# Softmax row sums of a decoder layer: one 128x32-block reduction on VectorE and one small matmul in place of five transposes, and the last two halves' sums taken from GpSimd

## The chip, the core and the metric

One NeuronCore of a Trainium2 chip runs the whole layer. TensorE (PE; its weight loads are shown as PEld) does matmuls and transposes into PSUM, ScalarE (ACT) and VectorE (DVE) read PSUM and SBUF, GpSimd (POOL) here works on SBUF alone, and SyncE (SP) issues nearly all DMAs. Each engine runs its own program in order and waits on semaphores. The metric is the device time of one execution in microseconds (us). A difference of less than about 0.2% can't be told from none for this kernel.

## What is computed

```python
x = layernorm(x + self_attention(x))
kv = concatenate([context, x], axis=1)              # 1601 + 256 rows, 4 batches
q = rms_norm(x @ Wq); k = rms_norm(kv @ Wk); v = kv @ Wv
# 8 key/value heads of width 128, 4 query heads on each
scores = einsum('bhgqd,bhkd->bhgqk', q, k) / sqrt(128)
probs = softmax(scores, axis=-1)
x = layernorm(x + einsum('bhgqk,bhkd->bhgqd', probs, v) @ Wo)
x = layernorm(router_ffn(x))                        # 64 experts, top 8
```

The change touches the denominator of `softmax`: for each query, the sum of the exponentials over all 1857 keys.

## The kernel before

**Tiles, halves, units.** A unit is one key/value head of one batch (`UNITS` 32, index `v`). Each has two halves (`HALVES` 64, index `p`): two query heads times 256 queries, so 512 columns. The 1857 keys are `NJ` 15 tiles (`j`) of 128 rows, the last of 65. A score tile `t = 15 p + j` has keys on the partitions and queries along the row, so a softmax sum runs across partitions and over 15 tiles.

**The order.** It is written by hand as steps `s`, one score tile each, and every engine goes through the same steps in its own program. At step `s`: PE does `scores(s)`, then the jobs of `fill(s)`, then `pv(s - 20)`. ACT does `exp(s - 18)` (twice for most tiles: `P_hi` rounded, then the full value into `row`), then `copy_scores(s)`. DVE does `shift(s - 18)` (subtracts the maximum spread in `Mb_ps`), `raise_max(s - 1)` and drains the PSUM results of the step before. POOL does `lo(s - 18)` (`P_lo` = full value minus `P_hi`) and `add(s - 18)`. Two score banks tie PE to DVE: `scores(s)` waits for `raise_max(s - 2)`. A ring of 21 score rows ties all to POOL: `copy_scores(s)` waits until tile `s - 21` was split and added. Tiles in `FULL` (j = 6, 7, 14 in the last two batches) are not split: they cost POOL no `lo`, and PE one fp32 matmul (two passes) in place of three.

**The fill jobs** repeat every 30 steps; `c = (s + 20) mod 30` is the place in this cycle. Projections of keys (`KV`) and queries (`Q`), transposes of keys (`KT`) and queries (`QT`), the maximum (`MT`), and output projections (`O`, p, t) stand there. They take turns in two PSUM banks `F_ps`, and a job waits until the second one before it is drained. Projections for the last unit end before step 940, score tiles end at 959, the last `pv` stands in step 979.

**Row sums.** POOL adds 15 tiles into `acc[p % 2]` (L902 the first pair, L906 the others): 14 instructions of 128x512 a half. Job `AT` (L1130, step 15 p + 35, c = 10 or 25) has PE transpose `acc` in four pieces; DVE reduces the result to `sums` 128x4 (L1730) and takes the reciprocal `rinv` (L1732). Job `RT` (L1137, two steps later) transposes `rinv` to 4x128; DVE copies it to `rrow` (L1752), SP stores it (L733) and reads it back spread over all partitions as `rinv_spread` (L740). `divide(p)` (L1815) and `OT_low(p)` (L1819) on DVE, with ACT's `OT_high` between, make the operands of `O`. After the last `O` come the layer norm, the router and the store of the last batch, one after the other.

## Time and profile before

| | |
|---|---|
| median of 3 runs | 2812.35 us (2811.64 to 2814.04) |
| the profiled execution | 2814.29 us, of which the instructions span 2812.5 us |
| PE busy | 2717.2 us, 97% |
| POOL busy | 2353.4 us, 84% |
| DVE busy | 2123.2 us, 75% |
| ACT busy | 2101.7 us, 75% |
| mean granted TensorE clock | 0.986 of 2.4 GHz |

The shares are averages over the whole program. PE is nearly full until about 2660 us; after that POOL is, and from 2767 us on the program is a single chain of short steps. A matmul's shown duration overlaps the next one's, so its cost is the distance between starts. The same holds, by some 0.1 us, for DVE and ACT.

### The profile page before, as it was taken

To read this page: it belongs to the slowest core of one execution; us is meant where nothing else is said; L and a number is where in the kernel's file an instruction comes from. 1 tells how busy PE (TensorE), PEld (TensorE's weight loads), DVE (VectorE), ACT (ScalarE), POOL (GpSimd) and SP (SyncE) were. 2 spreads that over 40 slices of the span, in tenths; PEclk is the share of its full clock that TensorE was granted. 3 is DMA by queue.
4 is the path that set the end of the run, shared out by engine and by line. 5 is a ranking of instruction groups with operands and counts; after the bars stand their busy time and mean duration, and the time that the engine had idled before them with its cause. 6 is when DMAs were issued, how large, how long until landed. Compare 5 with 4: busy or idle time off the path is not lost.

```text
span 2812.5 us, 48040 instructions
## 1 busy us (share of the span) xinstructions
PE 2717.2 (97%) x14812; PEld 2218.6 (79%) x14812; DVE 2123.2 (75%) x3532; ACT 2101.7 (75%) x4201; POOL 2353.4 (84%) x2320
## 2 busy tenths in 40 slices
PE   7899999999999999999999999999999999999975
PEld 5778778777878888888888888888888888888853
DVE  5577787877777877777777877777777878787873
ACT  3587777777777778777778887787787778777761
POOL 4299999898788888878889888888898888888893
PEclk9999999999999999999999999999999999999995
DMA  7656565565555454555545555554455445344310
GB/s 234 237 196 212 198 210 199 200 216 185 171 188 202 158 179 164 182 180 197 178 152 189 169 184 176 181 184 160 159 174 173 154 160 179 127 162 150 117 42 26
DMA packets 159435, 485.65 MB, mean 173 GB/s; under 512 B 16839, under 2 KB 27849, under 8 KB 159182
## 3 DMA queue, kind: packets, MB, share of 16 engines
q1 hardware_dynamic: 157592, 481.01, 50.9%
q8 instruction: 121, 1.98, 0.3%
q10 hardware_dynamic: 1590, 1.58, 0.2%
q14 instruction: 132, 1.08, 0.1%
HBM read 403.09 MB, written 79.43 MB: 172 GB/s over the span
## 4 chain that ended last, share of the span: by engine, by line
PE 82%; POOL 7%; issue 5%; DVE 3%; ACT 2%; DMA 1%; SPq 0%; ACTq 0%; POOLq 0%; DVEq 0%
PE K_ps L971 9%; PE K_ps L973 9%; PE K_ps L972 9%; PE OT_ps L1001 7%; PE S_ps L971 7%; PE S_ps L973 7%; PE S_ps L972 7%; PE OT_ps L971 5%; PE OT_ps L972 5%; PE OT_ps L973 5%; POOL acc L906 4%; PE F_ps L971 2%; PE F_ps L972 2%; PE F_ps L973 2%; POOL P_lo L888 2%
## 5 line engine op out<-in xcount | busy, mean ns | idle before, releaser
L906 POOL TENSOR_TENSOR acc<-acc,scores 128x512 f32<-128x512 f32 (+1 forms) x832 | 1105.3, 1328 | 53.0 <-ACT scores L1323 25.4
L888 POOL TENSOR_TENSOR P_lo<-scores,P_hi 128x512 fp32r<-128x512 f32 x672 | 891.8, 1327 | 215.4 <-ACT scores L1323 214.5
L1663 DVE SCALAR_TENSOR_TENSOR running_max<-S_ps,rk,running_max 128x512 f32<-128x512 f32 (+1 forms) x896 | 669.7, 747 | 304.7 <-ACT scores L1309 302.2
L1309 ACT ACTIVATE scores<-S_ps,rk 128x512 f32<-128x512 f32 (+1 forms) x960 | 652.5, 680 | 139.6 <-PE S_ps L973 121.3
L1647 DVE TENSOR_TENSOR scores<-scores,Mb_ps 128x512 f32<-128x512 f32 (+1 forms) x960 | 648.7, 676 | 135.5 <-PE Mb_ps L1127 135.4
L1322 ACT ACTIVATE P_hi<-scores 128x512 fp32r<-128x512 f32 x672 | 422.9, 629 | 265.3 <-DVE scores L1647 183.6
L1323 ACT ACTIVATE scores<-scores 128x512 f32<-128x512 f32 (+1 forms) x960 | 596.6, 622 | 15.2 <-DVE scores L1647 12.8
L971 PE MATMUL S_ps<-QT_hi,KT_hi 128*128 128x512 f32 (+1 forms) x960 | 496.2, 517 | 11.9 <-DVE running_max L1663 10.1
L971 PE MATMUL K_ps<-Wkv_hi,kvT 128*128 128x256 f32 (+1 forms) x1664 | 470.4, 283 | 2.4 <-DVE kvT L1713 2.4
L973 PE MATMUL K_ps<-Wkv_hi,kvT 128*128 128x256 f32 (+1 forms) x1664 | 470.7, 283 | 0.0
L972 PE MATMUL K_ps<-Wkv_lo,kvT 128*128 128x256 f32 (+1 forms) x1664 | 469.6, 282 | 0.0
L973 PE MATMUL S_ps<-QT_hi,KT_lo 128*128 128x512 f32 (+1 forms) x960 | 379.8, 396 | 0.0
L972 PE MATMUL S_ps<-QT_lo,KT_hi 128*128 128x512 f32 (+1 forms) x960 | 378.6, 394 | 0.0
L971 PEld LDWEIGHTS K_ps<-Wkv_hi,kvT 128*128 128x128 f32 (+1 forms) x1664 | 310.2, 186 | 22.5 <-DVE kvT L1713 2.9
L972 PEld LDWEIGHTS K_ps<-Wkv_lo,kvT 128*128 128x128 f32 (+1 forms) x1664 | 310.1, 186 | 20.2
L971 PE MATMUL OT_ps<-P_hi,V_hi 128*128 128x512 f32 x672 | 289.8, 431 | 31.0 <-POOL P_lo L888 30.6
L973 PEld LDWEIGHTS K_ps<-Wkv_hi,kvT 128*128 128x128 f32 (+1 forms) x1664 | 310.4, 187 | 0.0
L1001 PE MATMUL OT_ps<-scores,V_full 128*128 128x512 f32 (+1 forms) x576 | 297.7, 598 | 0.0
L971 PEld LDWEIGHTS S_ps<-QT_hi,KT_hi 128*128 128x128 f32 (+1 forms) x960 | 177.6, 185 | 114.1 <-DVE running_max L1663 44.5
L972 PE MATMUL OT_ps<-P_lo,V_hi 128*128 128x512 f32 x672 | 266.1, 396 | 0.0
L973 PE MATMUL OT_ps<-P_hi,V_lo 128*128 128x512 f32 x672 | 265.6, 395 | 0.0
L972 PEld LDWEIGHTS S_ps<-QT_lo,KT_hi 128*128 128x128 f32 (+1 forms) x960 | 178.2, 186 | 93.5 <-issue 64.7
(226 smaller groups left out, 4637.5 us busy)
## 6 DMA issues: line engine op xcount, KB each, us to landing
kvT<-kvT_scratch SPq DMA_DIRECT2D x403, 512.0 KB, 3.8
Wq_hi<-weight_halves_scratch SPq DMA_DIRECT2D x48, 512.0 KB, 5.3
Wq_lo<-weight_halves_scratch SPq DMA_DIRECT2D x48, 512.0 KB, 6.6
Wo_hi<-weight_halves_scratch SPq DMA_DIRECT2D x48, 512.0 KB, 4.7
Wo_lo<-weight_halves_scratch SPq DMA_DIRECT2D x48, 512.0 KB, 5.7
kvT_scratch<-built SPq DMA_DIRECT2D x45, 512.0 KB, 4.4
rinv_spread<-rinv_scratch SPq DMA_DIRECT2D x64, 256.0 KB, 4.9
Wkv_hi<-weight_halves_scratch SPq DMA_DIRECT2D x24, 512.0 KB, 5.6
```

Source lines behind the costliest of these rows:

```text
L888: e.tensor_tensor(P_lo[n % PB][0:r, :], prob(t)[0:r, :], f(P_hi[n % PB][0:r, :]), ALU.subtract)\
L906: e.tensor_tensor(a[0:r, :], a[0:r, :], prob(t)[0:r, :], ALU.add).then_inc(s_acc, 1)
L971: e.matmul(out, l_hi, r_hi, start=first, stop=False)
L972: e.matmul(out, l_hi, r_lo, start=False, stop=False)
L973: return e.matmul(out, l_lo, r_hi, start=False, stop=last)
L1001: ins = e.matmul(OT_ps[:], V_full[v % 2][0:r, FULL[v].index(j), :], row[t % RING][0:r, :], start=first, stop=last)
L1309: e.activation(row[s % RING][0:r, :], S_ps[s % 2][0:r, :], ACT.Copy, scale=rk[0:r, v % 2, j:j + 1])\
L1322: e.activation(P_hi[n % PB][0:r, :], d, ACT.Exp)
L1323: e.activation(d, d, ACT.Exp).then_inc(s_p, 1)
L1647: e.tensor_tensor(d, d, Mb_ps[0:r, :], ALU.add).then_inc(s_d, 1)
L1663: e.scalar_tensor_tensor(a, src, k, a, ALU.mult, ALU.max).then_inc(s_top, 1)
```

## The change

**In every half** `RT` is gone, and `AT` is another job. DVE reduces `acc` (in SBUF, 128x512) straight to `block_totals` 128x16: `tensor_reduce` over 32 columns at a time with `apply_transpose=True`, which turns each 32x32 block first, so that the sum runs over 32 keys for each of 512 queries. This stands in DVE's step before `AT`'s (`sum_blocks`). PE then multiplies `block_totals` with `same_in_block` (128x32, ones where partition and column agree modulo 32), which adds the four groups of partitions: one fp32 matmul with a 16x32 result. DVE takes its reciprocal into `rrow` 16x32. Store, spread, `divide`, `OT_high` and `OT_low` stand two steps earlier.

**In half 62** six tiles (j = 2, 4, ..., 12) are no longer added by POOL; DVE reduces each by blocks (`sum_tile`, in the step after the exponential) into a part of `sq`, which the sums of squares no longer need. **In half 63** this holds for all 15 tiles, and ACT zeroes the unused rows of the last tile's buffer once. A short reduction over the 7 or 15 partial results (`sum_blocks`) makes `block_totals`.

**Output projections.** `O` of half 61 moves from steps 961 and 963 to 959 and 960, `O` of half 62 from 981 and 983 to 975 and 976. The loads of `Wo` that follow them on SP move too (L686).

```diff
+    SUMMED = [[] for p in range(HALVES - 2)] + [[2, 4, 6, 8, 10, 12], list(range(NJ))]
+    ADDED = [NJ * p + j for p in range(HALVES) for j in range(1, NJ) if j not in SUMMED[p]]
+    LATE = [p for p in range(HALVES) if len(SUMMED[p]) == NJ]
+    ADD_AT = {t: n for n, t in enumerate(ADDED)}
...
-            12: [("RT", 2 * v - 3)],
...
-            27: [("RT", 2 * v - 2), ("QT", v, 1)],
+            27: [("QT", v, 1)],
...
+        if v == UNITS:
+            jobs = [x for x in jobs if x[0] != "O" or x[1] != HALVES - 3]
+            jobs += {19: [("O", HALVES - 3, 0)], 20: [("O", HALVES - 3, 1)]}.get(c, [])
+        if v == UNITS + 1:
+            jobs = [x for x in jobs if x[0] != "O" or x[1] != HALVES - 2]
+            jobs += {5: [("O", HALVES - 2, 0)], 6: [("O", HALVES - 2, 1)]}.get(c, [])
...
-        return [x[1] for x in fill(s - 6) if x[0] == "RT"]
+        return [x[1] for x in fill(s - 6) if x[0] == "AT"]
...
-        chunk = {5: ("Wkv", v + 1, 0), 11: ("Wq", v + 1, 0), 13: ("Wq", v + 1, 1), 14: ("Wo", v - 2, 1),
-                 24: ("Wo", v - 1, 0)}.get(c)
+        chunk = {5: ("Wkv", v + 1, 0), 11: ("Wq", v + 1, 0), 13: ("Wq", v + 1, 1), (7 if v > UNITS else 14): ("Wo", v - 2, 1),
+                 (21 if v == UNITS else 24): ("Wo", v - 1, 0)}.get(c)
...
+    def summed_tile(t):
+        return t % NJ in SUMMED[t // NJ]
...
+    BLOCKS = []
+    for s in STEPS:
+        if 0 <= s - WAIT - 1 < NS and summed_tile(s - WAIT - 1):
+            BLOCKS.append(s - WAIT - 1)
+        BLOCKS += [("acc", x[1]) for x in fill(s + 1) if x[0] == "AT" and SUMMED[x[1]] and x[1] not in LATE]
+    BLOCK_AT = {x: n for n, x in enumerate(BLOCKS)}
...
-        sums = sb("sums", [P, 2, 4])
-        rinv = sb("rinv", [P, 2, 4])
-        rrow = sb("rrow", [4, P])
+        sums = sb("block_totals", [P, 2, 16])
+        same = sb("same_in_block", [P, 32])
+        rrow = sb("rrow", [16, 32])
...
-                e.wait_ge(s_fr, F_AT["RT", p] + 1)
-                e.dma_start(rsd[p % 2].rearrange("(i q) -> i q", q=P), rrow[:]).then_inc(s_rd, 16)
+                e.wait_ge(s_fr, F_AT["AT", p] + 1)
+                e.dma_start(rsd[p % 2].rearrange("(i q) -> i q", q=32), rrow[:]).then_inc(s_rd, 16)
...
-                if j == 0:
+                if t not in ADD_AT:
...
-                        e.wait_ge(s_ff, F_AT["AT", p - 2] + 1)
+                        e.wait_ge(s_bt, p - 1)
...
-            def turn_sums(p):
-                e.wait_ge(s_acc, acc_no(NJ * p + NJ - 1))
+            def add_blocks(p):
+                if p == 0:
+                    e.wait_ge(s_same, 1)
+                e.wait_ge(s_bt, p + 1)
                 out = take(("AT", p))
-                for i in range(4):
-                    ins = e.transpose(out[:, i * P:(i + 1) * P], acc[p % 2][:, i * P:(i + 1) * P], ident[:])
-                ins.then_inc(s_ff, 1)
-
-            def turn_reciprocals(p):
-                e.wait_ge(s_ri, p + 1)
-                out = take(("RT", p))
-                e.transpose(out[0:4, 0:P], rinv[:, p % 2, :], ident[:]).then_inc(s_ff, 1)
+                e.matmul(out[0:16, 0:32], sums[:, p % 2, :], same[:], start=True, stop=True).then_inc(s_ff, 1)
...
+                    if summed_tile(t):
+                        e.wait_ge(s_bs, BLOCK_AT[t] + 1)
+                    else:
+                        e.wait_ge(s_acc, ADD_AT[t + 1 if t % NJ == 0 else t] + 1)
+                if r < P and p in LATE:
+                    e.activation(row[s % RING][TAIL // 32 * 32:P, :], row[s % RING][TAIL // 32 * 32:P, :], ACT.Copy,
+                                 scale=0.0).then_inc(s_z, 1)
+                    e.wait_ge(s_z, LATE.index(p) + 1)
...
+            e.reduce_sum(same[:], ident[:].rearrange("p (i a) -> p a i", a=32), AX.X).then_inc(s_same, 1)
...
-                    e.reduce_sum(sums[:, p % 2, :], out.rearrange("p (i k) -> p i k", k=P), AX.X).then_inc(s_fr, 1)
-                    e.wait_ge(s_fr, F_AT[job] + 1)
-                    e.reciprocal(rinv[:, p % 2, :], sums[:, p % 2, :]).then_inc(s_ri, 1)
+                    if p:
+
+                        e.wait_ge(s_rd, 16 * p)
+                    e.reciprocal(rrow[:], out[0:16, 0:32]).then_inc(s_fr, 1)
...
-                elif job[0] == "RT":
-                    p = job[1]
-                    if p:
-
-                        e.wait_ge(s_rd, 16 * p)
-                    e.tensor_copy(rrow[:], out[0:4, 0:P]).then_inc(s_fr, 1)
...
+            def sum_tile(t):
+                p, j = divmod(t, NJ)
+                e.wait_ge(s_p, t + 1)
+                e.tensor_reduce(blocks_of(p)[:, SUMMED[p].index(j), :], prob(t).rearrange("p (j a) -> p j a", a=32), AX.X,
+                                ALU.add, apply_transpose=True).then_inc(s_bs, 1)
+
+            def sum_blocks(p):
+                if p >= 2:
+
+                    e.wait_ge(s_ff, F_AT["AT", p - 2] + 1)
+                added = acc[p % 2][:].rearrange("p (j a) -> p j a", a=32)
+                if not SUMMED[p]:
+                    e.wait_ge(s_acc, ADD_AT[NJ * p + NJ - 1] + 1)
+                    e.tensor_reduce(sums[:, p % 2, :], added, AX.X, ALU.add, apply_transpose=True).then_inc(s_bt, 1)
+                    return
+                n = len(SUMMED[p])
+                if p in LATE:
+                    e.wait_ge(s_bs, BLOCK_AT[NJ * p + NJ - 1] + 1)
+                else:
+                    e.wait_ge(s_acc, ADD_AT[NJ * p + NJ - 1] + 1)
+                    e.tensor_reduce(blocks_of(p)[:, n, :], added, AX.X, ALU.add, apply_transpose=True).then_inc(s_bs, 1)
+                    e.wait_ge(s_bs, BLOCK_AT["acc", p] + 1)
+                    n += 1
+                e.reduce_sum(sums[:, p % 2, :], blocks_of(p)[:, 0:n, :].rearrange("p k j -> p j k"), AX.X).then_inc(s_bt, 1)
...
+                if 0 <= s - WAIT - 1 < NS and summed_tile(s - WAIT - 1):
+                    sum_tile(s - WAIT - 1)
+                for x in fill(s + 1):
+                    if x[0] == "AT":
+                        sum_blocks(x[1])
```

How this moves instructions is shown at three places. **PE**, an `AT` job in the middle of the program (the score and value matmuls around it are those of `scores` and `pv`), before:

```order
L973 MATMUL K_ps<-Wkv_hi,kvT 128x256
L1134 MATMUL F_ps<-ident,acc 128x128 x4
L971 MATMUL OT_ps<-P_hi,V_hi 128x512
L972 MATMUL OT_ps<-P_lo,V_hi 128x512
L973 MATMUL OT_ps<-P_hi,V_lo 128x512
```

and now:

```order
L995 MATMUL K_ps<-Wkv_hi,kvT 128x256
L1157 MATMUL F_ps<-same_in_block,block_totals 16x32
L993 MATMUL OT_ps<-P_hi,V_hi 128x512
L994 MATMUL OT_ps<-P_lo,V_hi 128x512
L995 MATMUL OT_ps<-P_hi,V_lo 128x512
```

One matmul stands where four transposes stood; the fifth, two steps later, has nothing in its place.

**DVE**, the sums of half 60 (L1647 and L1671 are `shift`, L1663 and L1687 `raise_max`), before:

```order
L1757 TENSOR_TENSOR y<-y,F_ps 128x512
L1647 TENSOR_TENSOR scores<-scores,Mb_ps 128x512
L1663 SCALAR_TENSOR_TENSOR running_max<-S_ps,rk,running_max 128x512
L1647 TENSOR_TENSOR scores<-scores,Mb_ps 128x512
L1663 SCALAR_TENSOR_TENSOR running_max<-S_ps,rk,running_max 128x512
L1730 TENSOR_REDUCE sums<-F_ps 128x4
L1732 RECIPROCAL rinv<-sums 128x4
L1719 TENSOR_TENSOR KT_lo<-F_ps,KT_hi 128x512
```

and now:

```order
L1776 TENSOR_TENSOR y<-y,F_ps 128x512
L1844 TENSOR_REDUCE block_totals<-acc 128x16
L1671 TENSOR_TENSOR scores<-scores,Mb_ps 128x512
L1687 SCALAR_TENSOR_TENSOR running_max<-S_ps,rk,running_max 128x512
L1671 TENSOR_TENSOR scores<-scores,Mb_ps 128x512
L1687 SCALAR_TENSOR_TENSOR running_max<-S_ps,rk,running_max 128x512
L1757 RECIPROCAL rrow<-F_ps 16x32
L1743 TENSOR_TENSOR KT_lo<-F_ps,KT_hi 128x512
```

The reduction moved two steps ahead, in front of two `raise_max`, and only a small reciprocal is left behind them.

**DVE in the last half**, around the division of half 62, before (nothing but `shift` stands there for the tiles of half 63):

```order
L1752 COPY rrow<-F_ps 4x128
L1647 TENSOR_TENSOR scores<-scores,Mb_ps 128x512 x5
L1815 TENSOR_TENSOR OT_n<-OT_n,rinv_spread 128x512
L1647 TENSOR_TENSOR scores<-scores,Mb_ps 128x512 x2
L1819 TENSOR_TENSOR OT_lo<-OT_n,OT_hi 128x512
```

and now:

```order
L1671 TENSOR_TENSOR scores<-scores,Mb_ps 128x512
L1834 TENSOR_REDUCE sq<-scores 128x16
L1859 TENSOR_TENSOR OT_n<-OT_n,rinv_spread 128x512
L1671 TENSOR_TENSOR scores<-scores,Mb_ps 128x512
L1834 TENSOR_REDUCE sq<-scores 128x16
L1671 TENSOR_TENSOR scores<-scores,Mb_ps 128x512
L1863 TENSOR_TENSOR OT_lo<-OT_n,OT_hi 128x512
L1834 TENSOR_REDUCE sq<-scores 128x16
L1671 TENSOR_TENSOR scores<-scores,Mb_ps 128x512
L1834 TENSOR_REDUCE sq<-scores 128x16
```

Each `shift` now has a block reduction beside it on DVE. On POOL half 62 has 12 `lo` and 8 adds where it had 12 and 14, and half 63 has 12 `lo` and no add.

## Rows read from the trace of the kernel before

**Rows 1.** Windows: us; busy us of PE, PEld, DVE, ACT, POOL; clock; DMA share, GB/s.

```profile
1300.00:1800.00 500.00, 499.72 (x2802) 418.08 (x2801) 384.43 (x633) 397.24 (x802) 438.48 (x441) 1.00 0.53 177
...
2700.00:2750.00 50.00, 37.35 (x133) 23.46 (x131) 36.16 (x50) 31.30 (x56) 49.28 (x40) 0.91 0.16 53
```

**Rows 2.** Waits of PE's weight loads, 300 to 2600 us: total, times, longest.

```profile
PEld S_ps L971 <- DVE running_max L1663: 38.1, 104, 2.3
```

**Rows 3.** Timeline of PE around AT and RT of half 33: start, duration, what.

```profile
1549.21 0.60 PE L1134 MATMUL F_ps<-ident,acc 128*128 128x128 f32 x4
1549.56 0.48 PE L971 MATMUL OT_ps<-P_hi,V_hi 128*128 128x512 f32 x1
1549.88 0.39 PE L972 MATMUL OT_ps<-P_lo,V_hi 128*128 128x512 f32 x1
1550.11 0.39 PE L973 MATMUL OT_ps<-P_hi,V_lo 128*128 128x512 f32 x1
...
1555.19 0.27 PE L1140 MATMUL F_ps<-ident,rinv 128*4 128x128 f32 x1
...
1555.53 0.40 PE L972 MATMUL OT_ps<-P_lo,V_hi 128*128 128x512 f32 x1
```

**Rows 4.** Timeline of PE, small fp32 matmuls of the router (8, two passes each).

```profile
2222.48 1.90 PE L1161 MATMUL F_ps<-self_qkv,w_stage 128*128 128x64 f32 x16
2224.19 0.48 PE L971 MATMUL OT_ps<-P_hi,V_hi 128*128 128x512 f32 x1
```

**Rows 5.** DVE's lines: duration ns min/median/max, first and last start us.

```profile
L1730 DVE TENSOR_REDUCE sums<-F_ps x64: 678/681/693, 178.2 to 2768.2; 128x4 f32<-128x512 f32 x64
...
L1671 DVE TENSOR_REDUCE ss_k<-sq x128: 541/679/689, 48.3 to 2674.5; 128x4 f32<-128x512 f32 x96, 128x3 f32<-128x384 f32 x32
...
L1815 DVE TENSOR_TENSOR OT_n<-OT_n,rinv_spread x64: 680/954/5920, 197.8 to 2778.1; 128x512 f32<-128x512 f32 x64
```

**Rows 6.** Timeline of POOL where it takes up half 62, and at its last split.

```profile
2699.34 2.54 POOL L888 TENSOR_TENSOR P_lo<-scores,P_hi 128x512 fp32r<-128x512 f32 x2
...
2762.66 1.25 POOL L888 TENSOR_TENSOR P_lo<-scores,P_hi 128x512 fp32r<-128x512 f32 x1
```

**Rows 7.** Timeline of DVE in halves 62 and 63 (idle before, and releaser).

```profile
2695.73 0.69 DVE L1647 TENSOR_TENSOR scores<-scores,Mb_ps 128x512 f32<-128x512 f32 x1 [3.23 <-PE Mb_ps L1127]
...
2703.41 0.66 DVE L1647 TENSOR_TENSOR scores<-scores,Mb_ps 128x512 f32<-128x512 f32 x1
2703.99 0.74 DVE L1663 SCALAR_TENSOR_TENSOR running_max<-S_ps,rk,running_max 128x512 f32<-128x512 f32 x1
2704.65 0.68 DVE L1757 TENSOR_TENSOR y<-y,F_ps 128x512 f32<-128x512 f32 x1
...
2729.63 1.28 DVE L1647 TENSOR_TENSOR scores<-scores,Mb_ps 128x512 f32<-128x512 f32 x2 [3.32 <-PE Mb_ps L1127]
...
2741.47 5.92 DVE L1815 TENSOR_TENSOR OT_n<-OT_n,rinv_spread 128x512 f32<-128x512 f32 x1 [1.31 <-DMA rinv_spread<-rinv_scratch]
```

**Rows 8.** Timeline of ACT, the exponentials of one tile in half 61.

```profile
2687.97 0.62 ACT L1322 ACTIVATE P_hi<-scores 128x512 fp32r<-128x512 f32 x1
2688.49 0.62 ACT L1323 ACTIVATE scores<-scores 128x512 f32<-128x512 f32 x1
```

**Rows 9.** Timeline of PE in half 63.

```profile
2743.20 0.80 PE L971 MATMUL OT_ps<-P_hi,V_hi 128*128 128x512 f32 x1 [0.85 <-POOL P_lo L888]
2743.79 0.63 PE L972 MATMUL OT_ps<-P_lo,V_hi 128*128 128x512 f32 x1
2744.22 0.63 PE L973 MATMUL OT_ps<-P_hi,V_lo 128*128 128x512 f32 x1
```

**Rows 10.** Timeline of all engines after the last tile.

```profile
2767.11 1.06 PE L1134 MATMUL F_ps<-ident,acc 128*128 128x128 f32 x4
...
2770.54 0.26 SPq L733 DMA_DIRECT2D rinv_scratch<-rrow  x1
...
2778.10 0.69 DVE L1815 TENSOR_TENSOR OT_n<-OT_n,rinv_spread 128x512 f32<-128x512 f32 x1 [5.33 <-DMA rinv_spread<-rinv_scratch]
```

More of the change, by code:

```diff
@@ L186, in real @@
                 return True
-            return 0 <= job[1] < (HALVES if job[0] in ("RT", "O", "MT", "AT") else UNITS)
+            return 0 <= job[1] < (HALVES if job[0] in ("O", "MT", "AT") else UNITS)
         return [x for x in jobs if real(x)]
     def divided(s):
-        return [x[1] for x in fill(s - 6) if x[0] == "RT"]
+        return [x[1] for x in fill(s - 6) if x[0] == "AT"]
     def splits(s):
@@ L301, in x_no @@
         return TILE_NO[b, n]
-    def acc_no(s):
-        p, j = divmod(s, NJ)
-        return (NJ - 1) * p + j
+    def summed_tile(t):
+        return t % NJ in SUMMED[t // NJ]
     def split_tile(t):
@@ L520, in layer @@
         s_mb = sem("negated_max_spread")
-        s_ri = sem("row_reciprocal")
+        s_same = sem("same_in_block")
+        s_z = sem("last_tile_rows_zeroed")
+        s_bs = sem("block_sums")
+        s_bt = sem("block_totals")
         s_rd = sem("row_reciprocals_stored")
@@ L561, in xrow_of, with blocks_of @@
             return row[0] if k < CTX and k % 2 else xrow[:]
+        def blocks_of(p):
+            at = p % 2 * 256
+            return sq[:].rearrange("p h d -> p (h d)")[:, at:at + NJ * 16].rearrange("p (k j) -> p k j", k=NJ)
         def bank(table, label):
@@ L807, in _ @@
                 for x in fill(s - 1):
-                    if x[0] == "RT":
+                    if x[0] == "AT":
                         store_reciprocals(x[1])
                 for x in fill(s - 3):
-                    if x[0] == "RT":
+                    if x[0] == "AT":
                         spread_reciprocals(x[1])
@@ L899, in add @@
                     if p >= 2:
-                        e.wait_ge(s_ff, F_AT["AT", p - 2] + 1)
+                        e.wait_ge(s_bt, p - 1)
                     e.tensor_tensor(a[:], prob(t - 1)[:], prob(t)[:], ALU.add).then_inc(s_acc, 1)
                     return
-                e.wait_ge(s_acc, acc_no(t - 1))
+                e.wait_ge(s_acc, ADD_AT[t])
                 e.tensor_tensor(a[0:r, :], a[0:r, :], prob(t)[0:r, :], ALU.add).then_inc(s_acc, 1)
@@ L1213, in _ @@
                     elif x[0] == "AT":
-                        turn_sums(x[1])
+                        add_blocks(x[1])
                     elif x[0] == "FR":
@@ L1224, in _ @@
                         mix(x[1], x[2])
-                    elif x[0] == "RT":
-                        turn_reciprocals(x[1])
                     else:
@@ L1307, in copy_scores @@
                         e.wait_ge(s_pv, t + 1)
-                    e.wait_ge(s_acc, acc_no(t + 1 if t % NJ == 0 else t))
+                    if summed_tile(t):
[6 more added lines that the diff above has]
+                    e.wait_ge(s_z, LATE.index(p) + 1)
                 e.activation(row[s % RING][0:r, :], S_ps[s % 2][0:r, :], ACT.Copy, scale=rk[0:r, v % 2, j:j + 1])\
@@ L1514, in _ @@
             e.wait_ge(s_pad, 5)
+            e.wait_ge(s_id, 2)
+            e.reduce_sum(same[:], ident[:].rearrange("p (i a) -> p a i", a=32), AX.X).then_inc(s_same, 1)
             e.wait_ge(sa_w, 32)
@@ L1837, in _ @@
                     OT_low(p)
+                if 0 <= s - WAIT - 1 < NS and summed_tile(s - WAIT - 1):
+                    sum_tile(s - WAIT - 1)
+                for x in fill(s + 1):
+                    if x[0] == "AT":
+                        sum_blocks(x[1])
                 for p in divided(s):
```

## The prediction

> **What bounds the kernel now.** I read the stretches first. In 500 us of the middle of the program PE is busy 499.72 us, POOL 438.48, ACT 397.24 and DVE 384.43, at the full clock [rows 1]: PE bounds, and its matmuls follow each other without a gap. PE is not alone, though: its weight loads waited 104 times, 38.1 us in all, for DVE's running maximum [rows 2]. In the last 50 us before 2750 this has turned: POOL is busy 49.28 of 50 us, PE only 37.35 [rows 1], and PE waits for `P_lo` before a value matmul [rows 9]. From 2767 us on a chain of single steps is left: turn the sums, invert, store, spread (a DMA that DVE waits 5.33 us for), divide, project, normalise, route [rows 10]. So there are three stages, and the change has a part in each.
>
> **Part 1: five transposes a half less on PE.** Without `AT` the first value matmul behind it would start at 1549.21 and the second 0.23 us later. They start at 1549.56 and 1549.88 [rows 3]. The second is 0.44 us late, and that is the cost of four transposes. For `RT` the second value matmul should start at 1555.42 and starts at 1555.53: 0.11 us. Together 0.55 us a half.
>
> The new matmul isn't in the trace. The nearest is the router's: 16 passes with 128 columns of weights and 64 moving take 1.71 us, 0.107 each [rows 4]. Two such passes and the 0.09 us that the first fp32r matmul behind a transpose loses (0.32 where 0.23 is usual, [rows 3]) make 0.30 us, an upper bound, since 16 columns of weights and 32 moving are less. The lower bound is one pass like `RT`'s, 0.11. I take 0.20, between. Net 0.345 us a half.
>
> It counts where PE bounds. Half 61's sum falls in POOL's stage, so 61 sums (0 to 60) count: 61 x 0.345 = **21 us** (15 to 27 by the bounds).
>
> What else moves here: DVE loses the PSUM reduction of 0.68 us [rows 5] with a reciprocal and a copy, and gains a reduction of `acc`, two steps earlier. The plain reduction of 128x512 from SBUF takes 0.679 us (L1671, [rows 5]); I take that for the block reduction. DVE ends a little less loaded. Queued behind the new wait for POOL's last add are `shift` and `raise_max`, on which PE's scores hang. The add is normally done two steps before, so I cost the wait at nothing; the cover is POOL's idle time of 61 us in the 500 [rows 1]. `acc` is 128x512 behind DVE's own `y` drain, and PE has 0.69 us of scores in front of `AT`: just enough for 0.6 us. `divide` and `OT_low` two steps earlier collide with other POOL instructions than now; 0.68 us alone, 0.954 in the median and 5.92 at worst [rows 5]. The DMA in front of `divide` keeps as many steps as it had. I cost both moves at nothing, since DVE has the idle time, but they take it at another place: plus or minus 8 us for the waits of part 1, because 38.1 us of them exist to be made smaller or larger.
>
> For the block reduction itself the Trainium skill, in Vector Engine (DVE) Microarchitecture Reference, section 3.8, says that the 32x32 array that transposes the input keeps one element per cycle per lane, which would leave the reduction at the price of the plain one. No row here shows it; if it holds, the rival of the slow reduction below falls.
>
> **Part 2: half 62 and half 63.** POOL takes up half 62 at 2699.34 [rows 6]. Before that, everything shifts by part 1.
>
> Half 62 up to the first `shift` of half 63: this `shift` waits for the spread maximum, which PE makes behind `pv` of tile j = 12 of half 62, hence behind its `lo`. POOL has 11 `lo` and 11 adds to there, 22 x 1.26 [rows 6] = 27.7 us, and the `shift` came at 2729.63 [rows 7], 2.6 us after that. Now it is 17 instructions, 21.4 + 2.6: 6.3 us less. But DVE has its own list from its first `shift` of half 62 at 2695.73: 15 `shift` at 0.6, 13 maxima at 0.66, 4 drains of `y` at 0.6 [rows 7], one reduction of the maximum and seven block reductions at 0.6, `divide` and `OT_low` at 1.1 each: 27.3 us, and some 2.5 us for the two banks of scores that it still waits on. That ends at 2725.5. So the saving is 2729.6 - 2725.5 = **4.1 us** (1.5 to 6.3).
>
> Half 63: from 2729.63 to the end of the last `lo`, 2763.91, it takes 34.3 us now, 26 POOL instructions. Without the adds DVE leads: a `shift` and a block reduction per tile, 1.2 us, 1.27 with the wait for the two exponentials (0.52 + 0.62, [rows 8]). 13 tiles x 1.27 = 16.5 us; the sums of half 62 (0.6 + 0.3) and a reciprocal, 1.1; `divide` 1.1 to 1.7 and `OT_low` 1.1, with 1 us of waiting for the DMA and ACT between them; one drain 0.6; then the last split tile's own way through `shift`, exponentials and `lo`, 0.7 + 1.2 + 1.3 with semaphores. That is 25 us, so **9.3 us** less (6 to 12). The `divide` of 5.92 us [rows 7] was DVE shut out by a POOL with a backlog of adds. Now POOL gets its work from DVE tile by tile and runs dry, so I don't expect it again. The first `O` of half 62 now waits on PE for `OT_low`, with the last `pv`s behind it. PE's 12 matmuls there were hidden in a DMA's time, and they are hidden again if PE has its full clock: 2.8 us in an idle engine. At half the clock, which the pitch of 0.43 us in [rows 9] shows for this place (0.23 is that of the full clock, [rows 3]), two `O` and four `pv` are 9 us, and up to 2.5 us stick out.
>
> ACT's zeroing of a few rows happens once: nothing, in ACT's idle time. So does the one small reduction that makes `same_in_block`, beside the loads of the opening. The moved `Wo` loads stand on SP before the store of the reciprocals, and their condition is met by then.
>
> **Part 3: behind the last tile.** From the end of the last `lo` to the store of the reciprocals 6.6 us pass now: 3.2 to the transposes at 2767.11 [rows 10], then four transposes, a reduction, a reciprocal, a transpose behind the first `O` of half 62, a copy behind a drain, and the store at 2770.54 [rows 10]. Now 3.2, one matmul (0.3) and one reciprocal (0.2): 3.7. Saved **2.9 us** (2 to 3.5). Store and spread stay at 7.6 us (2770.54 to 2778.10, [rows 10]), the rest as it was.
>
> **Sum.** 21 + 4.1 + 9.3 + 2.9 = 37.3 us off the execution's 2814.29 us: 2777.0. The span was 2812.5 us and the execution has 1.8 around it; the median of the runs is 1.9 us below this execution. On the median: 2812.35 - 37.3 = 2775 us, 1.3% faster.
>
> **Rivals.**
> - *The gain of part 1 is eaten by DVE* (2787 us). PE already waits for the maximum; a reduction of 0.6 us in front of two `raise_max`, and `divide` moved to another place among short steps, could take half of the 21 us, and DVE and PE at half the clock could leave the last halves 2 to 3 us worse than summed. For it: [rows 2]. Against: DVE has 116 us idle of 500 [rows 1] and has less to do.
> - *The new matmul costs only 0.11 and DVE's lighter load takes waits away* (2762 us): 27 us in part 1, 8 us of the 38.1, and 17 us in the rest. For it: waits stand where the old reduction stood before a drain of keys.
> - *The block reduction costs about twice a plain one* (2790 us): 0.6 us more, 21 times in the last halves, 12.6 us; in the batches it is just within the 0.7 us slack, some 2 us. Nothing in the trace excludes it, as no reduction there transposes.
> - *Slower: the block reduction takes 2.7 us, four times the plain one* (2898 us). Then DVE stops for 2 us more in every half; 0.7 of that is slack, and 61 x 1.3 = 79 us arrive at PE through the two score banks, and 21 x 2.04 = 43 us in the last halves; less the 37 us. It decides from an excess of about 1 us: 61 x 0.3 + 21 = 39 us cancel the gain.
> - *The change does not do what it says*: another engine holds the last halves, and part 1 is all below 0.2%. PE's full row of matmuls speaks against it.
>
> **How the numbers follow.** My forecast, 2766 to 2784 us, 0.50. Eaten by DVE 0.17; the larger gain 0.14; the twice-as-dear reduction 0.10; slower 0.05; no effect 0.04. The range that leaves out the slow case, no effect and the ends of the outer two is 2761 to 2792 us. Faster by over 0.2% (what a measurement of this kernel can tell from none): 0.91; within 0.2% 0.04; slower 0.05.
>
> **What the profile after would show.** Part 1: the second value matmul behind the new `AT` 0.2 us late in place of 0.44, and the same place of the program near 2600 us some 20 us earlier; its reduction at 0.68 us; waits for the running maximum near 38 us. Part 2: DVE, no longer POOL, nearly full in the last 40 us of tiles; the first `shift` of half 63 about 30 us behind half 62's; a `divide` under 2 us. Part 3: 3.7 us from the last `lo` to the store. I am wrong if the block reduction is much over 0.68 us, if PE shows new waits for `block_totals` or the maximum, or if PE at half the clock ends last in half 63.

## The result

| | |
|---|---|
| median of 4 runs | 2784.10 us (2781.45 to 2786.27) |
| the kernel before, 4 runs | 2811.99 us (2811.07 to 2814.04) |
| ratio | 0.9899, 95% interval 0.9887 to 0.9912 |

The changed kernel is 1.0% faster, by 27.9 us. The forecast was 2775 us, a gain of 37.3, and its range reached from 2761 to 2792.

The page's first part, busy time and share of the span, of the kernel after:

```profile
span 2782.6 us, 47574 instructions
...
PE 2699.7 (97%) x14620; PEld 2190.5 (79%) x14620; DVE 2126.8 (76%) x3491; ACT 2098.3 (75%) x4202; POOL 2326.1 (84%) x2300
```

Windows of after, with the columns of [rows 1]:

```profile
1300.00:1800.00 500.00, 499.67 (x2773) 414.44 (x2772) 380.81 (x623) 398.14 (x806) 438.81 (x440) 1.00 0.53 178
2700.00:2750.00 50.00, 36.29 (x125) 22.09 (x123) 40.04 (x66) 30.47 (x54) 31.45 (x25) 0.90 0.22 74
2720.00:2730.00 10.00, 7.91 (x20) 4.73 (x21) 8.99 (x16) 6.33 (x12) 7.99 (x7) 0.66 0.08 26
2730.00:2740.00 10.00, 8.26 (x30) 4.95 (x28) 9.43 (x16) 7.32 (x13) 6.45 (x5) 1.00 0.01 2
```

PE still fills the middle. In the last 50 us POOL has gone from 49.28 to 31.45 us busy, and near 2735 DVE leads with 9.43 of 10. That is the picture that the prediction drew. The sizes of its terms are another matter. The table takes each stretch from the same events in the two traces: the first `shift` of half 62 and of half 63, the end of the last `lo`, the store of the reciprocals, the division of half 63, the end of the span.

| stretch | before, us | after, us | gain | forecast |
|---|---|---|---|---|
| start to half 62 | 2695.73 | 2686.80 | **8.9** | 21 |
| half 62 | 33.90 | 30.38 | 3.5 | 4.1 |
| half 63, to the last `lo` | 34.28 | 24.15 | 10.1 | 9.3 |
| to the store | 6.63 | 2.44 | 4.2 | 2.9 |
| store to division | 7.56 | 4.36 | **3.2** | 0 |
| the rest | 34.4 | 34.5 | -0.1 | 0 |
| sum | | | 29.9 | 37.3 |

Three of the events of after, DVE's first `shift` of half 62 and of half 63, and POOL's last two `lo`:

```profile
2686.80 0.69 DVE L1671 TENSOR_TENSOR scores<-scores,Mb_ps 128x512 f32<-128x512 f32 x1 [2.81 <-PE Mb_ps L1149]
...
2717.18 1.28 DVE L1671 TENSOR_TENSOR scores<-scores,Mb_ps 128x512 f32<-128x512 f32 x2 [0.81 <-PE Mb_ps L1149]
...
2738.79 2.54 POOL L910 TENSOR_TENSOR P_lo<-scores,P_hi 128x512 fp32r<-128x512 f32 x2
```

Part 1 gave less than half of its 21 us, and 3.2 us came from a place that was to stay as it was. (29.9 is the difference of the two profiled spans, 27.9 that of the medians. Of the 8.9 us, 0.8 lie before score tile 20, where the two kernels still do the same: that is the spread of single profiles, and no gain.)

### The profile page after: what moved, and what is told of

The parts are those of the page before. It is cut to its first block, busy times and chain, and to the rows that moved or that the text cites. A ratio compares the mean times of both kernels' runs of the same rounds, so it can differ in the third digit from the quotient of the medians.

```text
span 2782.6 us, 47574 instructions
## 1 busy us (share of the span) xinstructions
PE 2699.7 (97%) x14620; PEld 2190.5 (79%) x14620; DVE 2126.8 (76%) x3491; ACT 2098.3 (75%) x4202; POOL 2326.1 (84%) x2300
## 4 chain that ended last, share of the span: by engine, by line
PE 78%; POOL 7%; issue 6%; DVE 5%; ACT 2%; DMA 1%; SPq 0%; POOLq 0%; DVEq 0%; ACTq 0%
PE K_ps L993 9%; PE K_ps L995 9%; PE K_ps L994 9%; PE OT_ps L1023 7%; PE S_ps L993 7%; PE S_ps L995 6%; PE S_ps L994 6%; PE OT_ps L993 5%; PE OT_ps L994 4%; PE OT_ps L995 4%; POOL acc L928 4%; POOL P_lo L910 2%; PE F_ps L993 2%; PE F_ps L994 2%; PE F_ps L995 2%
## 5 line engine op out<-in xcount | busy, mean ns | idle before, releaser
L928 POOL TENSOR_TENSOR acc<-acc,scores 128x512 f32<-128x512 f32 x813 | 1068.5, 1314 | 50.7 <-ACT scores L1345 23.3
L910 POOL TENSOR_TENSOR P_lo<-scores,P_hi 128x512 fp32r<-128x512 f32 x672 | 902.6, 1344 | 220.3 <-ACT scores L1345 219.2
L1687 DVE SCALAR_TENSOR_TENSOR running_max<-S_ps,rk,running_max 128x512 f32<-128x512 f32 (+1 forms) x896 | 668.0, 745 | 272.6 <-ACT scores L1331 270.0
L1671 DVE TENSOR_TENSOR scores<-scores,Mb_ps 128x512 f32<-128x512 f32 (+1 forms) x960 | 645.6, 673 | 138.9 <-PE Mb_ps L1149 138.8
L993 PE MATMUL S_ps<-QT_hi,KT_hi 128*128 128x512 f32 (+1 forms) x960 | 495.6, 516 | 15.5 <-DVE running_max L1687 13.8
```

Source lines behind the costliest of these rows:

```text
L910: e.tensor_tensor(P_lo[n % PB][0:r, :], prob(t)[0:r, :], f(P_hi[n % PB][0:r, :]), ALU.subtract)\
L928: e.tensor_tensor(a[0:r, :], a[0:r, :], prob(t)[0:r, :], ALU.add).then_inc(s_acc, 1)
L993: e.matmul(out, l_hi, r_hi, start=first, stop=False)
L1671: e.tensor_tensor(d, d, Mb_ps[0:r, :], ALU.add).then_inc(s_d, 1)
L1687: e.scalar_tensor_tensor(a, src, k, a, ALU.mult, ALU.max).then_inc(s_top, 1)
```

## The price of the new matmul

PE around `AT` of half 33 in the kernel after, the counterpart of [rows 3] (start, duration, what; a PEld row is the load of weights):

```profile
1551.01 0.28 PE L995 MATMUL K_ps<-Wkv_hi,kvT 128*128 128x256 f32 x1
1551.22 0.11 PEld L1157 LDWEIGHTS F_ps<-same_in_block,block_totals 128*16 128x16 f32 x2
1551.22 0.23 PE L1157 MATMUL F_ps<-same_in_block,block_totals 128*16 128x32 f32 x2
...
1551.38 0.50 PE L993 MATMUL OT_ps<-P_hi,V_hi 128*128 128x512 f32 x1
...
1551.72 0.39 PE L994 MATMUL OT_ps<-P_lo,V_hi 128*128 128x512 f32 x1
```

`K_ps` matmuls follow each other at 0.12 us, so the first value matmul would start at 1551.13 without the job and the second, 0.23 later, at 1551.36. It starts at 1551.72: **0.36 us**, where I had taken 0.20 and given 0.30 as the upper bound. `RT` had cost 0.11 and its going shows whole (step c = 12 is 0.10 to 0.11 us shorter in every batch). Net 0.19 us a half in place of 0.345: 61 x 0.155 = 9.5 us of the missing 12.

Two runs ask what the 0.36 is made of. The first issues the matmul twice:

```diff
+                e.matmul(out[0:16, 0:32], sums[:, p % 2, :], same[:], start=True, stop=True)
                 e.matmul(out[0:16, 0:32], sums[:, p % 2, :], same[:], start=True, stop=True).then_inc(s_ff, 1)
```

> The small fp32 matmul of `AT` is issued twice in a row. It says what it costs in the stream: the second value matmul behind it stands 0.36 us late in the changed kernel, where I had taken 0.20. If the two passes are the price (0.08 each) and the rest is paid once for entering and leaving, the place grows by 0.16 us and the whole by 8 to 10 us; if a weight load that can't be drawn ahead is paid each time, by 0.25 to 0.35 us and 15 to 20 us.

Measured: 2788.40 us (2787.85 to 2788.96, 2 runs), ratio 0.9914 (0.9894 to 0.9933). The same place of its trace:

```profile
1553.02 0.28 PE L995 MATMUL K_ps<-Wkv_hi,kvT 128*128 128x256 f32 x1
...
1553.30 0.22 PE L1158 MATMUL F_ps<-same_in_block,block_totals 128*16 128x32 f32 x2
...
1553.79 0.40 PE L994 MATMUL OT_ps<-P_lo,V_hi 128*128 128x512 f32 x1
```

The second value matmul is at 0.77 us behind the last `K_ps` where it was at 0.71. A second fp32 matmul, two passes, costs 0.06 us here and 0.07 in the mean of step c = 10, less than either expectation, and 61 of them are the 4.3 us between the medians of the two kernels. So 0.29 of the 0.36 isn't the passes: by this count it is paid for going into the fp32 matmul and out again.

The second run makes it one fp32r matmul, so that it is of the kind around it. `block_totals` and `same_in_block` are written as fp32r; the sums lose their low bits by this (the lines that permit the rounding are left out here):

```diff
-        sums = sb("block_totals", [P, 2, 16])
-        same = sb("same_in_block", [P, 32])
+        sums = sb("block_totals", [P, 2, 16], F32R)
+        same = sb("same_in_block", [P, 32], F32R)
```

> `block_totals` and `same_in_block` are written rounded as fp32r, so that the small matmul is one pass of the same kind as its neighbours (the sums lose low bits by it). The doubled matmul had shown that two passes themselves are 0.07 us of the 0.36. Theory C (the remaining 0.29 us is the change between fp32 and fp32r matmuls and their weight loads): the place falls to under 0.15 us, step c = 10 from 3.18 to about 2.95 us, and the whole by 12 to 18 us. Theory D (it is the wait on DVE's semaphore and the short weight load, whatever the type): c = 10 stays within 0.08 us of 3.18 and the whole falls by less than 5 us.

Measured: 2773.22 us (2771.61 to 2774.84, 2 runs), ratio 0.9855 (0.9835 to 0.9875), some 11 us below after, a little less than theory C's 12 to 18 and far from theory D. Its trace at the same place:

```profile
1544.15 0.28 PE L995 MATMUL K_ps<-Wkv_hi,kvT 128*128 128x256 f32 x1
1544.15 0.10 PEld L1157 LDWEIGHTS F_ps<-same_in_block,block_totals 128*16 128x16 f32 x1
1544.27 0.18 PE L1157 MATMUL F_ps<-same_in_block,block_totals 128*16 128x32 f32 x1
1544.27 0.19 PEld L993 LDWEIGHTS OT_ps<-P_hi,V_hi 128*128 128x128 f32 x1
...
1544.61 0.40 PE L994 MATMUL OT_ps<-P_lo,V_hi 128*128 128x512 f32 x1
```

Expected without the job is 1544.27 + 0.23 = 1544.50, and it is 1544.61: 0.11 us, my lower bound. (That bound was `RT`'s price; that the two agree to the digit is chance.) The load rows tell where the rest had been. As fp32r the small matmul's weights are loaded at 1544.15, while the `K_ps` matmul streams, and the value matmul's at 1544.27, with the small one. As fp32 both loads wait: the first until 1551.22, 0.21 behind the start of `K_ps`, and the next until 1551.38. That a matmul of another kind breaks the overlap of loads and matmuls twice is what the rows show; why is not shown.

This is the step of the prediction that failed. It took the price from the router's fp32 matmuls [rows 4], 0.107 a pass, and those 16 passes stand in a row. A row pays the way in and out once; that is read off the doubled matmul, and wasn't measured on the router's row itself. My 0.09 for the way out was right in kind and about a third of the whole.

## The division two steps earlier

The other part of the loss I had written down at nothing, "plus or minus 8 us". DVE's lines of after (duration ns min/median/max), as in [rows 5]:

```profile
L1859 DVE TENSOR_TENSOR OT_n<-OT_n,rinv_spread x64: 648/1092/2752, 191.3 to 2748.1; 128x512 f32<-128x512 f32 x64
...
L1844 DVE TRANSPOSE_TENSOR_REDUCE block_totals<-acc x62: 692/703/712, 173.7 to 2690.6; 128x16 f32<-128x512 f32 x62
```

The block reduction is 0.70 us, always (the 21 of single tiles in the last halves, too: 0.64 to 0.71). Of these 83 reductions 13 ran wholly inside a POOL instruction of over 1 us, and none took more than 0.71. The division is 2.75 us at times. In the first 16 halves the divisions took 14.6 us over 0.68 each, where before they took 4.5. One of them, DVE, POOL and PE in the kernel after:

```profile
743.44 2.38 POOL L967 TENSOR_TENSOR Wo_lo<-w_stage,Wo_hi 128x1024 fp32r<-128x1024 f32 x1 [0.80 <-ACT Wo_hi L1478]
...
743.62 2.75 DVE L1859 TENSOR_TENSOR OT_n<-OT_n,rinv_spread 128x512 f32<-128x512 f32 x1
...
746.89 0.74 DVE L1687 SCALAR_TENSOR_TENSOR running_max<-S_ps,rk,running_max 128x512 f32<-128x512 f32 x1
...
747.68 0.51 PE L993 MATMUL S_ps<-QT_hi,KT_hi 128*128 128x512 f32 x1 [0.94 <-DVE running_max L1687]
```

Up to 828 us POOL splits weights, 128x1024 in 2.38 us. The new step puts the division 0.18 us behind such a split. DVE is held past the end of it, the maximum behind the division is late, and PE stands 0.94 us for it. Both instructions read two operands from SBUF. The Trainium skill (SBUF — State Buffer, Who interferes with whom) says that a VectorE instruction with two SBUF inputs contends with a GpSimd one that reads SBUF, and that one with at most one such input, outside the 2-port modes, does not. The trace agrees on both: 2.75 and 0.70 us.

The experiment gives halves 0 to 60 their old steps for the division, `OT_high` and `OT_low`, and leaves the last three as changed:

```diff
-        return [x[1] for x in fill(s - 6) if x[0] == "AT"]
+        return [x[1] for x in fill(s - 8) if x[0] == "AT" and x[1] < HALVES - 3] \
+            + [x[1] for x in fill(s - 6) if x[0] == "AT" and x[1] >= HALVES - 3]
```

> The change as it is, but `divide`, `OT_high` and `OT_low` stand in their steps of before for halves 0 to 60 (c = 18 and 3 for the division). Theory A (the earlier steps of the division ate part of the gain): in the changed kernel the division of odd halves takes 2.75 us in the first batch, where 0.68 was usual, and the PE step c = 17 there grew from 2.20 to 3.41 us; undone, the time falls by 6 to 11 us, to 2773 to 2778 us, and c = 17 is back at 2.2 us. Theory B (the block reduction in front of two running maxima ate it, the division is only where the delay shows): the time stays within 2 us of 2784, and PE waits as much for the running maximum.

Measured: **2776.79 us** (2775.70 to 2777.12, 4 runs), ratio 0.9873 (0.9856 to 0.9889), 7.3 below after, as theory A had it. Of the same half the division is now

```profile
742.53 0.68 DVE L1860 TENSOR_TENSOR OT_n<-OT_n,rinv_spread 128x512 f32<-128x512 f32 x1
```

and half 62 starts at

```profile
2677.62 0.69 DVE L1672 TENSOR_TENSOR scores<-scores,Mb_ps 128x512 f32<-128x512 f32 x1 [3.24 <-PE Mb_ps L1150]
```

9.2 us before the 2686.80 of after. The steps tell where. I measured each step by the distance from the end of the third score matmul of one tile to that of the next, and took the mean over a batch (steps 40 to 219, 220 to 459, 460 to 699 and 700 to 929); of 30 steps, two halves:

| us for two halves | before | after | division late |
|---|---|---|---|
| batch 0 | 84.37 | 84.76 | 83.82 |
| batch 1 | 82.59 | 82.68 | 82.21 |
| batch 2 | 81.46 | 81.10 | 81.06 |
| batch 3 | 83.74 | 82.68 | 82.68 |
| batch 0, step c = 17 | 2.20 | 3.41 | 2.20 |
| batch 0, step c = 19 | 2.66 | 2.07 | 2.65 |
| every batch, c = 10 | 3.27 | 3.18 | 3.18 |
| every batch, c = 25 | 2.26 | 2.14 | 2.14 |

The division at c = 17 costs 1.2 us and gives 0.6 back at c = 19. Of the 9.2 us at half 62, 7.4 have come about by step 270 (838 us in after), where the splits of weights end. Some 2.5 more come after them, up to 1470 us, at c = 5 and 19, and 0.8 of it goes again towards the end; what delays those steps is open.

That DVE's reduction before two `raise_max` should cost something has fallen for batches 0 to 2: with the reduction in its new place and the division in its old one, c = 17 is 2.20 as before, and the steps c = 9 and 24, where the reduction stands, are as long as before to 0.02 us.

## The 6.5 us that nobody had asked for

With the division late half 62 starts 18.1 us before that of the kernel before, and 61 x 0.19 is only 11.6. The steps show where the other 6.5 came from: some 4.7 in batch 3, 1.0 in batch 0, and 0.8 in the opening, where the kernels are alike. Batch 3 gained 1.06 us for two halves, where the two jobs explain 0.38. It sits at c = 27, 2.80 to 2.26, and c = 28, 3.02 to 2.80, and in batch 0 at c = 27, 2.55 to 2.30. DVE at such a place before, at 2411 to 2416 us, behind `AT` at c = 25:

```profile
2411.68 0.68 DVE L1730 TENSOR_REDUCE sums<-F_ps 128x4 f32<-128x512 f32 x1
...
2412.49 0.66 DVE L1719 TENSOR_TENSOR KT_lo<-F_ps,KT_hi 128x512 fp32r<-128x512 f32 x1
...
2413.96 1.10 DVE L1808 TENSOR_TENSOR self_x<-self_x 128x128 f32<-128x128 f32 x1
2414.98 1.24 DVE L1810 TENSOR_SCALAR self_small<-self_small 128x2 f32<-128x2 f32 x1
```

and with the change (the kernel with the late division):

```profile
2398.42 0.34 DVE L1758 RECIPROCAL rrow<-F_ps 16x32 f32<-16x32 f32 x1
2398.69 0.61 DVE L1744 TENSOR_TENSOR KT_lo<-F_ps,KT_hi 128x512 fp32r<-128x512 f32 x1
...
2400.11 0.42 DVE L1828 TENSOR_TENSOR self_x<-self_x 128x128 f32<-128x128 f32 x1
2400.46 1.24 DVE L1830 TENSOR_SCALAR self_small<-self_small 128x2 f32<-128x2 f32 x1
```

DVE is full here: the router's work for one half of the queries stands behind the sums, and the next score tile hangs on its end. In the 4 us from 2411.5 DVE was busy 3.93 of 4. Before, this step took 3.97 us at tile 847, now 2.84. From the first of these rows to `KT_lo` it was 0.81 us and is 0.27: that is the reduction that left, less what the wider reciprocal adds, 0.54. From the router's product `self_x` to the next row it was 1.02 and is 0.35, 0.67 less: it has two SBUF operands, and before it started 0.33 us into a POOL split of 1.28 us and ended behind it; now it starts 0.28 us before one POOL instruction ends and is through at the seam to the next. The two make 1.21, a little more than the 1.13. To test it I put, on top of the late division, a reduction of the old shape back into the drain of `AT`, into a spare tile that nobody reads:

```diff
+                    e.reduce_sum(spare[:, 0, 0:4], out.rearrange("p (i k) -> p i k", k=P), AX.X)
```

> On top of late_divide (2776.8 us), DVE's reduction of 128x512 from PSUM stands again where it stood before, in the drain of `AT`, for nothing. Part 1 brought more than PE's own saving: with the late division half 62 begins 18 us earlier, and 61 x (0.55 - 0.36) is only 12. Theory E (the other 6 us are DVE's: without the reduction the running maxima behind it come sooner, and PE's steps c = 27 and 28 of the last batch are 0.75 us shorter a pair): 4 to 7 us come back, 2781 to 2784 us, and c = 27 of the last batch rises from 2.26 to 2.6 us or more. Theory F (they come from elsewhere, the missing `RT` for one): less than 2 us, c = 27 stays.

Measured: 2785.32 us (2782.42 to 2786.66, 3 runs), ratio 0.9899 (0.9880 to 0.9919), 8.5 above the kernel with the late division alone. The place in its trace:

```profile
2405.18 0.68 DVE L1759 TENSOR_REDUCE spare<-F_ps 128x4 f32<-128x512 f32 x1
...
2407.47 1.08 DVE L1830 TENSOR_TENSOR self_x<-self_x 128x128 f32<-128x128 f32 x1
```

The 1.08 is back, c = 27 is 2.89 in batch 3 and 2.79 in batch 0. The direction is confirmed. The size is more than expected: c = 28 of batch 3 rises to 3.14, where the kernel before had 3.02. The kernel has the wider reciprocal and the block reduction on DVE as well, which may be why; that isn't shown.

The next run, again on top of the late division, doubles the block reduction in halves 0 to 61 (a second copy goes to a spare tile); the short sums of the last two halves' tiles are not doubled. It asks how much slack (time that DVE can lose without PE waiting) there is in front of `AT`:

```diff
+                    e.tensor_reduce(spare[:, 1, :], added, AX.X, ALU.add, apply_transpose=True)
                     e.tensor_reduce(sums[:, p % 2, :], added, AX.X, ALU.add, apply_transpose=True).then_inc(s_bt, 1)
```

> On top of late_divide (2776.8 us), the block reduction of `acc` is done twice in halves 0 to 61, first into an unused tile: 0.7 us more of DVE in front of two running maxima, and `AT` waits for it. This is the batches' share of my rival of a reduction twice as dear, which I had put at 2 us because of 0.7 us of slack. If the slack is there, 1 to 4 us more (2778 to 2781). If PE's place behind `raise_max` has none, most of 61 x 0.7 us arrives: 20 to 40 us more.

Measured: 2785.60 us (2784.79 to 2787.68, 3 runs), ratio 0.9904 (0.9884 to 0.9923), 8.8 more than without. Neither expectation holds, and the steps say why. For two halves batch 0 is 83.82, batch 1 82.19 and batch 2 81.06, which is what it was to 0.02 us: 0.7 us more of DVE cost nothing there. Batch 3 is 84.14 against 82.68 (c = 25 +0.26, c = 27 +0.60, c = 28 +0.61), 7 x 1.46 = 10.2 us. (The rest of the 12.0 us between the two profiled spans is 2.1 us in the opening, where the kernels are alike, and 0.6 in half 62, less 0.9 behind the last tile.) So the slack of "just enough" is there in the first three batches, and DVE has none in batch 3.

## The last halves

Two runs take the parts apart. The first leaves POOL all its additions:

```diff
-    SUMMED = [[] for p in range(HALVES - 2)] + [[2, 4, 6, 8, 10, 12], list(range(NJ))]
+    SUMMED = [[] for p in range(HALVES)]
```

> The change with POOL adding all tiles of all halves again (no tile is reduced by itself on DVE); the reduction of `acc` by blocks, the small matmul and the moved steps stay. If the last halves' gain (some 13 us up to the last `P_lo`) comes from POOL's 20 missing adds, the time rises by 12 to 15 us, to 2796 to 2799 us, and POOL is full to the end of half 63. If it comes from the moved output projections and divisions, it rises by less than 4 us.

Measured: 2799.57 us (2798.57 to 2802.49, 4 runs), ratio 0.9955 (0.9940 to 0.9970), 15.5 above after. Its division of half 62 is stretched again:

```profile
L1859 DVE TENSOR_TENSOR OT_n<-OT_n,rinv_spread x64: 677/1107/7558, 193.3 to 2763.7; 128x512 f32<-128x512 f32 x64
```

7.56 us at worst, 5.92 before [rows 5], 0.65 after:

```profile
2728.93 0.69 DVE L1834 TRANSPOSE_TENSOR_REDUCE sq<-scores 128x16 f32<-128x512 f32 x1
...
2730.12 0.69 DVE L1834 TRANSPOSE_TENSOR_REDUCE sq<-scores 128x16 f32<-128x512 f32 x1
2730.74 0.65 DVE L1859 TENSOR_TENSOR OT_n<-OT_n,rinv_spread 128x512 f32<-128x512 f32 x1
```

The pitch of `shift` and block reduction is 1.2 us a tile, as summed. So POOL's backlog was the bound of half 63, and its additions are worth 15.5 us together with what they do to the division: by the profiles 4.0 in half 62, 9.6 in half 63 and 1.8 from the last `lo` to the store. The late division with three more tiles (8, 10, 12 of half 61) summed by DVE:

```diff
-    SUMMED = [[] for p in range(HALVES - 2)] + [[2, 4, 6, 8, 10, 12], list(range(NJ))]
+    SUMMED = [[] for p in range(HALVES - 3)] + [[8, 10, 12], [2, 4, 6, 8, 10, 12], list(range(NJ))]
```

> Late division, and three tiles (j = 8, 10, 12) of half 61 are summed on DVE as well. POOL takes up half 62 behind half 61's adds; if POOL still bounds half 61, three adds of 1.26 us less bring 2 to 4 us (2773 to 2775 us). If DVE or PE bounds there by now, nothing, or up to 2 us more.

Measured: 2773.92 us (2772.94 to 2774.69, 4 runs), ratio 0.9857 (0.9841 to 0.9874): 2.9 below the two-half version, which ran on another chip, with intervals that overlap. In the profiled executions half 62 starts 1.3 us earlier and the last `lo` ends 0.7 earlier. A gain of a microsecond or two is likely, not proved.

The second part undone is the place of the output projections and of the `Wo` loads:

```diff
-        if v == UNITS:
-            jobs = [x for x in jobs if x[0] != "O" or x[1] != HALVES - 3]
-            jobs += {19: [("O", HALVES - 3, 0)], 20: [("O", HALVES - 3, 1)]}.get(c, [])
-        if v == UNITS + 1:
...
-        chunk = {5: ("Wkv", v + 1, 0), 11: ("Wq", v + 1, 0), 13: ("Wq", v + 1, 1), (7 if v > UNITS else 14): ("Wo", v - 2, 1),
-                 (21 if v == UNITS else 24): ("Wo", v - 1, 0)}.get(c)
+        chunk = {5: ("Wkv", v + 1, 0), 11: ("Wq", v + 1, 0), 13: ("Wq", v + 1, 1), 14: ("Wo", v - 2, 1),
+                 24: ("Wo", v - 1, 0)}.get(c)
```

> The change with the output projections of halves 61 and 62, and the loads of `Wo` that follow them, in their steps of before. In the changed kernel the spread of the last reciprocals took 4.4 us from store to division, 7.6 before. Theory A: the loads of `Wo` (two of 512 KB) ran beside the spread before; with the old steps they do so again, and 2.5 to 4 us come back (2786.5 to 2788), with a store to division of about 7.5 us. Theory B: the layout of 16 rows of 32 makes the store quick; then it stays near 4.4 us and the time within 1.5 us.

Measured: 2789.44 us (2786.15 to 2790.90, 4 runs), ratio 0.9916 (0.9901 to 0.9930), 5.3 above after. It is not where I looked: the time from store to division stays, as theory B had it, though its reason fails too. All engines after the last tile, kernel after (SPq is SP's queue, where DMAs are issued):

```profile
2743.13 0.23 PE L1157 MATMUL F_ps<-same_in_block,block_totals 128*16 128x32 f32 x2
...
2743.77 0.32 SPq L755 DMA_DIRECT2D rinv_scratch<-rrow  x1
2745.10 0.32 SPq L762 DMA_DIRECT2D rinv_spread<-rinv_scratch  x1
2748.13 0.69 DVE L1859 TENSOR_TENSOR OT_n<-OT_n,rinv_spread 128x512 f32<-128x512 f32 x1 [4.38 <-DMA rinv_spread<-rinv_scratch]
```

and the kernel with the old steps:

```profile
2747.07 0.32 SPq L749 DMA_DIRECT2D rinv_scratch<-rrow  x1
...
2748.39 0.32 SPq L756 DMA_DIRECT2D rinv_spread<-rinv_scratch  x1
...
2750.87 0.32 SPq L702 DMA_DIRECT2D Wo_hi<-weight_halves_scratch  x1
...
2751.48 0.69 DVE L1853 TENSOR_TENSOR OT_n<-OT_n,rinv_spread 128x512 f32<-128x512 f32 x1
...
2752.86 0.69 DVE L1857 TENSOR_TENSOR OT_lo<-OT_n,OT_hi 128x512 fp32r<-128x512 f32 x1 [0.70 <-ACT OT_hi L1353]
2755.93 0.61 PE L987 MATMUL F_ps<-Wo_hi,OT_hi 128*128 128x512 f32 x1 [5.09 <-issue]
```

From the store to the division it is 4.36 us in after, 4.41 with the old steps, 4.32 in the kernel whose additions stay on POOL (4.3 to 4.8 over all the runs), and 7.56 before [rows 10]. In the kernel before alone the two `Wo` loads of 512 KB are issued between the store, at 2770.54, and the spread:

```profile
2772.07 0.32 SPq L686 DMA_DIRECT2D Wo_hi<-weight_halves_scratch  x1
2772.44 0.43 SPq L686 DMA_DIRECT2D Wo_lo<-weight_halves_scratch  x1
2772.97 0.38 SPq L740 DMA_DIRECT2D rinv_spread<-rinv_scratch  x1
```

The spread goes out 2.43 us behind the store and takes 5.13. In the three others no `Wo` load stands between the two: 1.3 and 3.0. Theory B's reason, the layout of 16 rows of 32, falls by the kernel before itself: its sums of half 62, in the old layout and with no `Wo` load beside them, were stored at 2737.20, spread at 2738.37 and there at 2741.47, which is 1.17 and 3.1 us. With the old steps the spread, two steps earlier like all of the chain, is simply ahead of the loads. The loss there is another. From the last `lo` to the store it takes 4.04 us for 2.44: the last value matmuls stand at 0.43 us a pitch, at a granted clock of 0.50. And behind the division it takes 2.2 us more: the loads are now last, and the final projection, ready at 2753.6, starts at 2755.93 when `Wo` has landed.

## Point by point

The measured gain lies in the range, and in part by luck. Part 1's own bounds, 15 to 27 us, were missed by far, and 3.2 us that made up for some of it came from a place that the prediction had put at nothing.

- **Part 1, 21 us forecast, 8.9 measured.** The term that failed is the new matmul: 0.36 us, above the upper bound of 0.30, for 0.20 (9.5 us). The division that I had costed at nothing costs 9.2 us at half 62 (7.3 by the medians). The waits gave 6.5 us back, 0.8 of it the openings' spread, which I had not summed either. 21 - 9.5 - 9.2 + 6.5 = 8.8; the 6.5 is what remains when the other two are taken off, so that the sum comes out proves nothing. The division and the waits together, -2.7 us, are well within the "plus or minus 8"; the price of the matmul is outside its bounds.
- The rival "eaten by DVE" named the division among short steps and its 2787 us is the nearest of all to the result. Its mechanism was half right: the division, yes, for the most part by POOL's weight splits; the reduction in front of two `raise_max`, no. The sum of PE's waits for the maximum said nothing, 38.7 us where it was 38.1:

```profile
PEld S_ps L993 <- DVE running_max L1687: 38.7, 92, 3.1
```

- **The block reduction** is 0.70 us for 128x512, 0.02 over the plain one. What the Trainium skill says in Vector Engine (DVE) Microarchitecture Reference, section 3.8, that the transposing array keeps one element per cycle per lane, is borne out, and the rivals of the reduction twice and four times as dear fell.
- **Part 2** was right by steps: 3.5 for 4.1, and 24.15 us for the 25 of half 63. DVE led, the division was under 2 us, and PE's half clock came (0.66 in the window from 2720) and went (1.00 from 2730) without ending last. Two sums of the prediction are a little off: DVE's list for half 62 adds up to 27.0 us and not 27.3, and the rival with the larger gain comes to 2760 us and not 2762. Neither changes a verdict.
- **Part 3**, 4.2 for 2.9. I kept 3.2 us from the last `lo` to the small matmul; it is 1.8, since PE had half its clock there before and has all of it now, as the windows of that stretch show, first of before, then of after:

```profile
2763.90:2767.20 3.30, 3.24 (x6) 1.76 (x7) 0.00 (x0) 0.00 (x0) 2.50 (x3) 0.50 0.00 0
```

```profile
2741.30:2743.20 1.90, 1.82 (x7) 0.94 (x7) 1.62 (x3) 0.00 (x0) 0.03 (x1) 1.00 0.92 354
```

"Store and spread stay at 7.6 us" was wrong by 3.2: I had noted that the `Wo` loads now stand before the store (they are issued at 2738.99 and 2739.36), and not asked where they had stood and what they had done there.

## What beats both kernels

The late division and the one-pass matmul together (both diffs above):

> Both together: the division in its steps of before for halves 0 to 60, and the one-pass fp32r matmul. By theory C some 12 to 18 us below late_divide's 2776.8, at 2759 to 2765 us; by theory D 2772 to 2777 us.

Measured: **2766.07 us** (2762.16 to 2768.82, 4 runs), ratio 0.9829 (0.9814 to 0.9843), 1.7% below the kernel before. Over the late division alone it gains 10.7 us by the medians and 8.1 by the profiled spans, less than the 12 to 18 expected (1.7 us of the difference between the two figures are the openings): in batches 1 to 3 two halves are 0.35 to 0.47 us shorter, in batch 0 only 0.07 (c = 19 is 2.73 for 2.65, c = 27 2.42 for 2.30, c = 28 3.16 for 2.96). What holds batch 0 there is open. With exact fp32 sums the late division with three halves, 2773.92, is the best that was run.

## What to carry to other kernels

Price a small matmul by the distance between its neighbours in a stream of the same kind; a lone fp32 one among fp32r ones paid 0.29 us here for the way in and out, and a second one behind it did not pay it again. A moved instruction costs what it meets at its new place: look at what the engine that shares its operands' memory does in that very step, in each stage of the program. And of a load that is moved ask also where it had stood: its going can be the gain.
